# A conv layer's filter loads by stacked halves, and one more head split by batch pairs

## The reference

```python
x = x + experts(gn(x), gate_w, w1, w2, w3)       # 8 experts, top 2, F = 1024, D = 512
for w3, w7, w15, w_mix in three_layers:          # w_k: [512, 1, k], w_mix: [32, 96]
    v = gn(x)
    outs = [causal_depthwise_conv(v as [4, 512 channels, 512 tokens], w) for w in (w3, w7, w15)]
    y = concatenate(outs, axis=channels)         # 1536 channels, seen as 16 heads x 96
    x = x + einsum('blhm,dm->blhd', y, w_mix)
```

## Time and profile before

| | us |
|---|---|
| median of 3 runs | 1032.7 (1032.67 to 1033.59) |
| profiled execution | 1034.63 |
| its span | 1033.0 |
| TensorE (PE) busy | 992.5 (96%) |
| VectorE (DVE) busy | 498.2 (48%) |
| ScalarE (ACT) busy | 323.2 (31%) |
| GpSimd (POOL) busy | 255.8 (25%) |
| conv layers, each with its start | 115.5, 103.7, 108.8 |

### The profile page before, as it was taken

One profiled execution on the slowest core, in us unless ns is written; L12 is line 12 of the kernel. 1 busy time (PEld: TensorE's weight loads), 2 busy tenths in 40 slices (PEclk: granted clock), 3 DMA queues, 4 the chain that ended last, 5 costly groups with the idle time before them and its releaser, 6 DMA issues.

```text
span 1033.0 us, 14467 instructions
## 1 busy us (share of the span) xinstructions
PE 992.5 (96%) x5077; PEld 829.1 (80%) x5078; DVE 498.2 (48%) x660; ACT 323.2 (31%) x437; POOL 255.8 (25%) x359
## 2 busy tenths in 40 slices
PE   4989999999999999999999999968999999999998
PEld 3568888888888888888887888857988898889787
DVE  6763263145136246116337155146733896489411
ACT  2613252144144144125235244122511222122223
POOL 1011112121112112111212111112534245424531
PEclk9999999999999999999999999998999999999999
DMA  9576118934971994981893994975467747674668
GB/s 371 234 263 206 22 30 334 392 107 180 393 259 28 397 393 128 409 303 28 335 389 129 396 376 138 406 222 169 143 204 169 219 143 203 165 223 144 192 152 226
DMA packets 98786, 238.12 MB, mean 231 GB/s; under 512 B 10048, under 2 KB 64576, under 8 KB 83840
## 3 DMA queue, kind: packets, MB, share of 16 engines
q1 hardware_dynamic: 90528, 214.54, 57.6%
q0 software_dynamic: 8080, 23.07, 9.5%
q10 hardware_dynamic: 144, 0.07, 0.0%
HBM read 129.91 MB, written 111.94 MB: 234 GB/s over the span
## 4 chain that ended last, share of the span: by engine, by line
PE 75%; DMA 8%; DVE 6%; issue 5%; SPq 4%; ACT 1%; POOL 0%; ACTq 0%; DVEq 0%; POOLq 0%
PE gate_ps L1020 15%; PE up_ps L1020 15%; PE y_ps L1007 10%; PE head_ps L1598 6%; PE head_ps L1594 6%; PE head_ps L1595 6%; PE y_ps L1010 5%; DMA w_raw<-in_w13T 4%; PE hT_ps L1032 2%; SPq L460 2%; DMA ring<-filters 1%; PE xT_ps L997 1%; DMA rowed<-acc 1%; PE head_ps L1613 1%; PE head_ps L1614 1%
## 5 line engine op out<-in xcount | busy, mean ns | idle before, releaser
L1020 PE MATMUL gate_ps<-front 128*128 128x512 f32 x560 | 176.4, 396 | 2.2 <-DVE xT_lo L867 1.5
L1020 PE MATMUL up_ps<-front 128*128 128x512 f32 x560 | 173.2, 390 | 0.0
L1594 PE MATMUL head_ps<-split,ring 128*128 128x256 f32 (+1 forms) x459 | 158.9, 346 | 4.0 <-DMA ring<-filters 2.4
L1598 PE MATMUL head_ps<-split,ring 128*128 128x256 f32 (+1 forms) x459 | 155.3, 338 | 2.2 <-DVE split L1396 2.2
L1595 PE MATMUL head_ps<-split,ring 128*128 128x256 f32 (+1 forms) x459 | 153.8, 335 | 0.0
L882 DVE TENSOR_TENSOR hidden<-silu,up_ps 128x1024 f32<-128x1024 f32 x35 | 42.7, 1221 | 228.7 <-ACT silu L641 228.7
L1020 PEld LDWEIGHTS up_ps<-front 128*128 128x128 f32 x560 | 105.4, 188 | 22.3
L1020 PEld LDWEIGHTS gate_ps<-front 128*128 128x128 f32 x560 | 102.6, 189 | 22.8 <-DVE front L831 1.8
L528 POOL DMA_INDIRECT acc<-y_row,put x35 | 67.4, 1927 | 214.4 <-ACT y_row L629 214.4
L641 ACT ACTIVATE silu<-gate_ps 128x1024 f32<-128x1024 f32 x35 | 35.9, 1024 | 267.5 <-PE up_ps L1020 267.5
L1007 PE MATMUL y_ps<-w_hi,hT_hi 128*128 128x512 f32 x280 | 112.2, 401 | 1.2 <-ACT hT_hi L623 1.2
(11 more groups left out here) (198 smaller groups left out, 1435.1 us busy)
## 6 DMA issues: line engine op xcount, KB each, us to landing
filters<-rows SPq DMA_DIRECT2D x56, 1568.0 KB
w_raw<-in_w13T SPq DMA_DIRECT2D x32, 1024.0 KB, 16.4
ring<-filters SPq DMA_DIRECT2D x15, 1536.0 KB, 6.6
w_raw<-in_w2T SPq DMA_DIRECT2D x16, 1024.0 KB, 6.0
ring<-filters SPq DMA_DIRECT2D x144, 64.0 KB, 4.1
ring<-filters SPq DMA_DIRECT2D x12, 768.0 KB, 4.8
ring<-filters SPq DMA_DIRECT2D x15, 384.0 KB, 3.7
ring<-filters SPq DMA_DIRECT2D x9, 512.0 KB, 4.0
```

Of the source, the lines that this page charges most:

```text
L1020: last = nc.tensor.matmul(o[:, n, :], a[:, k, :], b[:, k, t, n * 512:(n + 1) * 512], start=(k == 0 and a is xT_hi and b is w13_hi), stop=( ...
L1594: nc.tensor.matmul(place, kernel_hi, x_hi, start=(u == 0 and a == 0), stop=False)
L1598: nc.tensor.matmul(place, kernel_hi, x_lo, start=False, stop=False)
```

## The change

1. `LAYER_ORDER`: head 2 goes from the full tasks to the paired ones, so that a layer has 9 full tasks and ends with heads 2, 3, 4, 5 for pair 0 and then for pair 1: 23 tasks. `TAIL`, `REDUCTIONS`, `RING_PLACE`, `STORES`, the places of `total` and the orders on VectorE and ScalarE follow.
2. The shared window's filters are loaded by two transfers of 128 rows (one for the low part, one for the high part, each for both units) in place of two of 64 rows with both parts. The left-over half is loaded by one transfer of 128 rows, low part above high part, in place of three.
3. The left-over half's products: hi (64 rows, the lower half of the array's rows) times the low part directly out of `split`, and [lo; hi] times `single`, which now holds the high part twice. For this the low part comes first in `filter_sb` and in the ring, the halves of `shared` change places, and `at_block` in the expert part moves by `LAGS` elements.

```diff
-LAYER_ORDER = ([(h, pair) for pair in range(2) for h in HEAD_ORDER[:3]] + [(h, None) for h in HEAD_ORDER[3:13]]
-               + [(h, pair) for pair in range(2) for h in (3, 4, 5)])
+LAYER_ORDER = ([(h, pair) for pair in range(2) for h in HEAD_ORDER[:3]] + [(h, None) for h in HEAD_ORDER[3:12]]
+               + [(h, pair) for pair in range(2) for h in (2, 3, 4, 5)])
-TAIL = LAYER_TASKS - 6
+TAIL = LAYER_TASKS - 8
-RING_PLACE = {11: 0, 12: 14, 6: 28, 13: 0, 14: 14, 15: 0, 10: 14, 7: 28, 8: 0, 9: 16, 0: 8, 1: 24, 2: 0, 3: 14, 4: 19, 5: 28}
+RING_PLACE = {11: 0, 12: 14, 6: 28, 13: 0, 14: 14, 15: 0, 10: 14, 7: 28, 8: 0, 9: 16, 0: 8, 1: 0, 2: 14, 3: 19, 4: 24, 5: 29}
-    RING_COUNT.append((_l + 1) * (len(head_runs(_h)) + 5))
+    RING_COUNT.append((_l + 1) * (len(head_runs(_h)) + 3))
-REDUCTIONS = ((8, range(11, 16), None), (12, range(6, 11), None), (15, range(0, 3), None),
-              (17, range(3, 5), 0), (18, range(5, 6), 0), (20, range(3, 5), 1), (21, range(5, 6), 1))
+REDUCTIONS = ((8, range(11, 16), None), (12, range(6, 11), None), (14, range(0, 2), None),
+              (17, range(2, 5), 0), (18, range(5, 6), 0), (21, range(2, 5), 1), (22, range(5, 6), 1))
-          (19, 0, 3, range(PAIR, BATCH)), (22, 3, 6, range(PAIR, BATCH)))
+          (19, 0, 2, range(PAIR, BATCH)), (23, 2, 6, range(PAIR, BATCH)))
...
                 at = (RING_PLACE[h] + head_windows(h) - 2) * 2 * P
-                for half, m in zip((1, 0), head_shared(h)):
-                    s, j, count = head_parts(h)[m]
-                    begin = SCALE_AT[s] + count * P
-                    sp.dma_start(ring[half * P // 2:(half + 1) * P // 2, at:at + 2 * P].bitcast(f32).rearrange("p (a n) -> p a n", n=P),
-                                 filter_rows[P // 2:P, 2 * (l * GROUPS + j):2 * (l * GROUPS + j + 1), begin:begin + P]).then_inc(ring_in[h], 16)
+                m = head_shared(h)[0]
+                s, j, count = head_parts(h)[m]
+                begin = SCALE_AT[s] + count * P
+                for part in range(2):
+                    sp.dma_start(ring[:, at + part * P:at + (part + 1) * P].bitcast(f32),
+                                 filter_rows[P // 2:P, 2 * (l * GROUPS + j) + part:2 * (l * GROUPS + j) + part + 3:2, begin:begin + P]
+                                 .rearrange("r u n -> u r n")).then_inc(ring_in[h], 16)
                 at += 2 * P
                 s, j, count = head_parts(h)[head_single(h)]
                 begin = SCALE_AT[s] + count * P
-                sp.dma_start(ring[:, at + P:at + 2 * P].bitcast(f32), filter_rows[:, 2 * (l * GROUPS + j) + 1, begin:begin + P]).then_inc(ring_in[h], 16)
-                for half in range(2):
-                    sp.dma_start(ring[half * P // 2:(half + 1) * P // 2, at:at + P].bitcast(f32),
-                                 filter_rows[P // 2:P, 2 * (l * GROUPS + j), begin:begin + P]).then_inc(ring_in[h], 16)
+                sp.dma_start(ring[:, at:at + P].bitcast(f32),
+                             filter_rows[P // 2:P, 2 * (l * GROUPS + j):2 * (l * GROUPS + j + 1), begin:begin + P].rearrange("r s n -> s r n")).then_inc(ring_in[h], 16)
...
-                pool.wait_ge(low_ok, piece)
                 nc.gpsimd.tensor_copy(moving(single[0:P // 2, at], pair, 0),
-                                      moving(split[P // 2:P, j, 1], pair, 0).bitcast(f32)).then_inc(single_ok, 1)
+                                      moving(split[P // 2:P, j, 0], pair, 0).bitcast(f32)).then_inc(single_ok, 1)
...
-                kernel_hi, kernel_lo = (ring[:, (2 * at + part) * P:(2 * at + part + 1) * P] for part in range(2))
-                x_both = moving(single[:, SINGLE_SLOT[h]], pair, a)
+                j = head_units(h)[head_single(h)][1]
+                kernel_both = ring[:, 2 * at * P:(2 * at + 1) * P]
+                pe.wait_ge(low_ok, l * len(PIECES) + PIECE_OF[j, pair] + 1)
+                nc.tensor.matmul(place, kernel_both[P // 2:P, :], moving(split[P // 2:P, j, 1], pair, a), start=False, stop=False)
                 pe.wait_ge(single_ok, 2 * (n + 1))
-                nc.tensor.matmul(place, kernel_hi, x_both, start=False, stop=False)
-                last = nc.tensor.matmul(place, kernel_lo, x_both, start=False, stop=True)
+                last = nc.tensor.matmul(place, kernel_both, moving(single[:, SINGLE_SLOT[h]], pair, a), start=False, stop=True)
                 last.then_inc(head_done, 1)
```

More of the change, by code:

```diff
@@ L296, in experts_part @@
             "p (j i c) -> p j i c", j=TOP_K, i=TILES)
-        at_block = late_rows[:, 0:TOP_K * TILES * COLUMNS].rearrange("p (j i c) -> p j i c", j=TOP_K, i=TILES)
+        at_block = late_rows[:, LAGS:LAGS + TOP_K * TILES * COLUMNS].rearrange("p (j i c) -> p j i c", j=TOP_K, i=TILES)
         weight_block = w2_lo[:, :, :].rearrange("p k n -> p (k n)")[:, TOP_K * TILES * COLUMNS:(1 + PARTS_OF_WEIGHT) * TOP_K * TILES * COLUMNS].rearrange(
@@ L612, in after_first @@
                         act.wait_ge(product_ok, e * 2 + (i - 1))
-                        nc.scalar.activation(filter_sb[:, i, 0].bitcast(f32r), filter_sb[:, i, 1], ACT.Copy).then_inc(filter_hi_ok, 1)
+                        nc.scalar.activation(filter_sb[:, i, 1].bitcast(f32r), filter_sb[:, i, 0], ACT.Copy).then_inc(filter_hi_ok, 1)
             def xT_high(g):
@@ L648, in _ @@
             for i in range(2):
-                nc.scalar.activation(filter_sb[:, i, 1].rearrange("p (a d) -> p a d", d=HD),
+                nc.scalar.activation(filter_sb[:, i, 0].rearrange("p (a d) -> p a d", d=HD),
                                      lasting.whole[:, None, 0:HD].to_broadcast([P, LAGS // HD, HD]), ACT.Copy, scale=0.0).then_inc(filter_zero, 1)
@@ L853, in after_first @@
                         last = nc.vector.tensor_tensor(
-                            filter_sb[:, i, 1, at:at + k * HD].rearrange("p (k d) -> p k d", d=HD),
+                            filter_sb[:, i, 0, at:at + k * HD].rearrange("p (k d) -> p k d", d=HD),
                             taps_sb[:, c, tap:tap + k].rearrange("p o k -> p (o k)")[:, :, None].to_broadcast([P, k, HD]),
@@ L861, in after_first @@
                     dve.wait_ge(filter_hi_ok, e * 2 + (i - 1))
-                    nc.vector.tensor_tensor(filter_sb[:, i, 1].bitcast(f32r), filter_sb[:, i, 1], filter_sb[:, i, 0],
+                    nc.vector.tensor_tensor(filter_sb[:, i, 0].bitcast(f32r), filter_sb[:, i, 0], filter_sb[:, i, 1],
                                             ALU.subtract).then_inc(filter_ok, 1)
@@ L1233, in share @@
                     pool.wait_ge(head_done, slot_free(l, i))
-                for half, j in ((1, 2 * tile), (0, 2 * tile + 1)):
+                for half, j in ((0, 2 * tile), (1, 2 * tile + 1)):
                     nc.gpsimd.tensor_copy(both_parts(shared[half * P // 2:(half + 1) * P // 2, slot], pair),
@@ L1317, in _ @@
                 base = (l - 1) * LAYER_TASKS
-                for k in range(TAIL + 3):
+                for k in range(TAIL + 4):
                     square(base + k)
@@ L1322, in _ @@
                     high(l, i)
-                square(base + TAIL + 3)
+                square(base + TAIL + 4)
                 high(l, 2)
-                square(base + TAIL + 4)
                 square(base + TAIL + 5)
+                square(base + TAIL + 6)
+                square(base + TAIL + 7)
                 high(l, 3)
@@ L1481, in _ @@
                 add(base + TAIL + 1)
-                reduce(part + 3, base + TAIL + 1, range(3, 5), 0)
                 add(base + TAIL + 2)
-                reduce(part + 4, base + TAIL + 2, range(5, 6), 0)
+                reduce(part + 3, base + TAIL + 2, range(2, 5), 0)
                 add(base + TAIL + 3)
+                reduce(part + 4, base + TAIL + 3, range(5, 6), 0)
+                add(base + TAIL + 4)
                 stats_begin(l, 0)
@@ L1490, in _ @@
                 low(l, 0)
-                add(base + TAIL + 4)
+                add(base + TAIL + 5)
                 norm(l, 2)
                 low(l, 1)
-                reduce(part + 5, base + TAIL + 4, range(3, 5), 1)
+                add(base + TAIL + 6)
                 low(l, 2)
-                add(base + TAIL + 5)
-                reduce(part + 6, base + TAIL + 5, range(5, 6), 1)
+                reduce(part + 5, base + TAIL + 6, range(2, 5), 1)
+                add(base + TAIL + 7)
+                reduce(part + 6, base + TAIL + 7, range(5, 6), 1)
                 norm(l, 3)
@@ L1588, in head @@
                     for a in range(count):
-                        kernel_hi, kernel_lo = (ring[:, (2 * at + part * count + a) * P:(2 * at + part * count + a + 1) * P]
+                        kernel_lo, kernel_hi = (ring[:, (2 * at + part * count + a) * P:(2 * at + part * count + a + 1) * P]
                                                 for part in range(2))
@@ L1601, in head @@
                 a = head_parts(h)[head_shared(h)[0]][2]
```

(4 more changed lines are left out.)

1 line of the change is left out of this document (removed).

## The result

The changed kernel takes 1136.76 us (median of 4 runs, 1135.48 to 1138.68) where the kernel before takes 1032.68 (1031.74 to 1033.59). The ratio is 1.1009, with a 95% interval of 1.0988 to 1.1031: 104 us slower, where 117 were forecast (1150), inside the range of 1100 to 1215.

The account below looks back on a forecast made before the run. TensorE, busy 96%, bounds the kernel before; two DMA engines then become the bound at 142 us a layer against 103.7: +38 a layer, +115 over three, +1 for the clock, from span 1033.0 to about 1150 us, range 1100 to 1215.

Parts of the forecast that it names:

- The form of the three transfers decides: Ring loads: a leading dimension of two puts each of the three transfers on the same two engines; +115 us.
- The sum for a layer: Conv layer on the two engines: 88 + 42 + 12 = 142 us, where TensorE needs 103.7.
- the trio: A head's three small transfers: 64 rows each at 28.7 ns, 5.5 us a head, 88 us a layer.
- The time without room in the ring: Loads waiting for a ring place: 10 us before head 13, 2 more before heads 12 and 15.
- The bulk: The two engines' share of each head's main filter load, 48 packets a head: 42 us a layer.
- Named waits of 100 us and more, 3 to 6 us each: Sign: TensorE released mostly by `ring<-filters`, 100 us or more in total, 3 to 6 us before heads 1 to 5.
- Landings of 8 us: Sign: the 64 KB ring transfers land at 8 us and more, where the median was 4.0.
- Rival (c): Left-over half's 64-row product: 0.10 us a switch, two a task, 69 tasks, 0 to +14 us; chance 0.06.
- Part one as good as nothing: Head 2 by pairs: +0.08 us a layer, small gains at split waits, other end changes under 0.5 us together.
- part two: Ring loads and left-over half's products: two transfers fewer a head, 1.2 us of SyncE's queue; the form of those left decides.
- Rival (b): All sixteen engines carry the transfers, but head 5's earlier due time eats the gain, 0.8 us late becomes 1.2: 1033; chance 0.04.
- The clock, +1 us: TensorE's clock falls in waits; slower products hide behind filters except pair 1's half tasks at layer end: +1 us in all.

Follow-up runs that it names:

- five: Changed kernel with the task order of the kernel before, no stacked transfer (four of 64 rows), product of 128 rows: 1032.41 us, ratio 0.9994.
- eight: As five, with all three transfers a head stacked: 1125.3 us, ratio 1.0886.
- three: As two, with the left-over half's product of 64 rows made one of 128 rows: 1042.13 us, ratio 1.0076.
- four: Changed kernel, transfers stacked as they are, with the product of 128 rows in place of 64: 1125.54 us, ratio 1.0892.
- nine: As five, with the left-over half's product on 64 rows as in the change: 1053.65 us, ratio 1.0203.
- ten: Changed kernel with the old task order, keeping three stacked transfers and the 64-row product: 1135.81 us, ratio 1.0998.
- two: Changed kernel with its three stacked transfers issued as four of 64 rows each, same data to the same places: 1057.62 us, ratio 1.0238.
- seven: As five, with only the shared window's two transfers stacked: 1068.51 us, ratio 1.0325.
- one: Four heads by pairs as in the changed kernel, with transfers, copy and product of the kernel before: 1052.28 us, ratio 1.0172.
- Twelve: As three, with two small transfers of 128 rows a head in place of four; shared and left-over windows get other filter rows: 1030.15 us, ratio 0.997.
- six: As five, with only the left-over window's transfer stacked: 1034.09 us, ratio 1.0002.
- eleven: As three, with the left-over window's transfer stacked, four issues a head for five: 1048.49 us, ratio 1.0149.

## Why the prediction was right, point by point

**The form of the three transfers decides: right.** The term was +115 us. Alone it is worth 93 (five to eight), 83 (three to four), 82 (nine to ten) or 79 (two against the changed kernel), in part less because what the pairs and the product of 64 rows add hides behind the same queue.

**The sum for a layer: total right, 142 against 139.9 us, terms off in both directions.** A packet of 512 bytes holds one of the two engines for 24.5 ns, not 28.7: the trio is 16 x 192 x 24.5 ns = 75 us, not 88. The packet itself lasts as forecast; by the prediction's formula, share x 16 x window / packets, the stretch at 951 gives 0.143 x 16 x 2 / 163 = 28.1 ns. But the formula counts the overlap of two packets on one engine twice, and when two engines work alone they overlap. The time without room in the ring was put at 12 us. The same DMA view shows all engines idle for 10.8 us ahead of head 13's load (second fence above), 3.1 at 896 and 4.8 at 984: 19. The bulk, put at 42 us, can be read in part: heads 0 to 4 start 6.0 to 6.2 us apart where 4.7 of trio and 1.2 of bulk make 5.9, and SyncE starts the loads with a bulk of 1024-byte packets 7.0 us apart (912.91 to 934.02 for three), where 4.7 and the forecast 2.4 make 7.1. That of the large heads is not read apart. 75 + 42 + 19 would be 136, so about 4 us of a layer are not accounted for. So the term that was mis-sized most is the packet's price, -13 us a layer; the gaps and the rest give 11 of them back. Against the forecast +38 in each layer stand +35, +36 and +32.

**Named waits of 100 us and more, 3 to 6 us each: wrong in size and kind.** 48.3 us are named, the longest 3.5. The second layer's +36.2 can be split: 19.3 us of ring waits, 23 x 0.39 = 9 of spacing about the 64 rows, and some 8 left. The 8 fit the clock, though nothing measures them alone: at 951 to 953 it is granted at 0.50, the level of 1.2 GHz, after a wait of 2.1 us, and products of 512 columns then start 0.43 us apart; in 957 to 984 it is 0.68 on the mean. The prediction had such slow products "hide behind the filters". That fits, but then what they fill is not named a wait. As to single waits, at heads 1 to 5 of the second layer they are 2.1, 0.7, 3.3, 3.3 and 2.0 us, for a load takes 6.0 us and not 6.9. The same shows in the runs: 63.4 us of named waits come with 93 us lost (eight), 63.1 with 92 (four), 25.0 with 36 (seven).

**Landings of 8 us: nearly.** The page of the changed kernel gives no landing for the loads of the ring, but its critical chain (the work that ended last, followed back) holds two, start and duration from the last issue of a load to its landing, head 5's in the second layer and the one of head 12 behind it:

```profile
968.43 7.56 DMA ring<-filters
...
989.57 10.31 DMA ring<-filters
```

At heads 0 to 4 of that layer 6.5 to 6.6 us lie between the start of the last issue and the product that needs it. The median before was 4.0. DMA share under 0.5 (0.42) and layers of about 140 us: right.

**Rival (c), the product of 64 rows: the mechanism was there and its price too low.** The bound from above was 0.20 us a task, 14 us; it is 0.39 by the rows and 21 us by experiment nine. The nearest row, the gate's products on 32 columns, gave 0.10 a switch; the first switch costs that, the change back 0.19, and 0.10 more falls on the next task's first product. "Under 5 us" on top of the main forecast is wrong: it is 11 us (four), because it hides only where TensorE waits behind it. Four and the changed kernel close the account: 69 x 0.39 = 27 us more spacing, 14.8 us less wait, 11.2 us more time.

**Part one as good as nothing: wrong, though the changed kernel hides it.** It adds 1 us on top of part two (ten), but 18 us by itself (one) and 8 to 10 with five issues a head (five to three; 8 by the ratios, as these two ran on different chips). Rival (b) counted the issues, 17 against 19, for loads of four issues, and so priced head 5's earlier due time at 0.4 us. It looked at the sum up to head 5 and not at the pace: four loads in a row feed half tasks of 1.7 us, so each may take SyncE 1.7 us, and it takes 3.8 with six issues and 3.2 with five. Twelve, at 1.6 us a load, ends the waits but one. (The price of an issue was read a little high: the six of head 3 in the earlier trace rows take 0.59 us each, not 0.63; over the run of 25 it was 0.61.)

**The clock, +1 us:** inside the split above; what it costs beyond the filters' own time no run isolates.

93, 21 and 10 add up to more than 104, since all three push on the same wait. Of the kernels here that compute the whole result, none beats the kernel before; part two's layout without a stacked transfer and with the product of 128 rows (five) equals it. A layout of `filter_rows` that holds the two halves of the stacked window one behind the other, so that one transfer with 128 as its first dimension moves them, would give twelve's queue with the right rows; it was not tried, and what writing that layout costs is open.

## What to carry to other kernels

Before transfers are merged, write down the first dimension of both patterns: three transfers of 64 KB with a leading two cost 79 to 93 us here, the same bytes with 64 in front, in one issue more, none in the old order. One such transfer alone was free in the old order and cost 6 us in the paired one. Count then what is left of the issuing queue where consumers are shortest: a load of six issues is 3.8 us of SyncE, and feeds no task of 1.7. A single product on fewer rows between full ones is no saving, since it streams the same columns and costs 0.3 to 0.4 us a time.

## What had not been expected of the hardware

**A backlog on two engines holds the issuing queue.** In the changed kernel's second layer, SyncE's queue (start, duration of the issue) with the two engines behind:

```profile
945.98 1.72 SPq L1176 DMA_DIRECT2D ring<-filters  x1
947.75 2.81 SPq L1183 DMA_DIRECT2D ring<-filters  x2
950.60 1.49 SPq L1189 DMA_DIRECT2D ring<-filters  x1
```

and after an idle stretch of the DMA engines:

```profile
988.03 0.37 SPq L1176 DMA_DIRECT2D ring<-filters  x1
988.45 1.08 SPq L1183 DMA_DIRECT2D ring<-filters  x2
989.57 4.90 SPq L1189 DMA_DIRECT2D ring<-filters  x1
```

The same pair of issues takes 1.08 us with the engines idle and 2.81 with a backlog; the third, just behind, 4.90. So the load of the next head is issued late too, and the fourteen idle engines can't run ahead with their part of its bulk. That the stacked issue is not dear by itself is seen at the pair for the shared window where that pair is not stacked: between 815 and 1000 us it takes 1.32 us on the mean in experiment five, which has no stacked transfer, and 1.68 and 1.73 in six and eleven, which have one other that is.

**How much of a late load is named a wait depends on the clock.** Heads 0 and 1 of the second layer both take 14 products of 512 columns, and each of their successors starts 6.0 us behind them (rows above). At the full clock, from 945.06, 2.06 us of that are named a wait; at 0.50, from 951.05, 0.70. The seven slow products, 0.43 us apart for 0.23, fill the rest.
